# A graph network on one core: the order of work in the first blocks of each layer

## The reference

```python
for l in range(4):
    m = x @ weight[l]
    agg = segment_sum(m[src], dst)
    gi = agg @ w_ih.T + b_ih
    gh = x @ w_hh.T + b_hh
    r = sigmoid(i_r + h_r); z = sigmoid(i_z + h_z)
    n = tanh(i_n + r * h_n)
    x = (1 - z) * n + z * x
```

## Time and profile before

| | us |
|---|---|
| median of 3 runs | 2386.22 |
| lowest and highest | 2385.95, 2386.53 |
| the profiled execution | 2388.24 |
| its span in the trace | 2386.5 |
| PE busy | 2235.7 (94%) |
| DVE busy | 2227.2 (93%) |
| ACT busy | 1902.0 (80%) |
| POOL busy | 1722.0 (72%) |

### The profile page before, as it was taken

The page is one execution under the profiler, slowest core; times in us unless marked ns, Lnnn a source line. Parts: engine busy times, 40 slices in busy tenths (PEclk is TensorE's granted clock), DMA queues, the critical chain, the costliest instruction groups (busy, mean ns, idle before and its releaser), DMA issues.

```text
span 2386.5 us, 49508 instructions
## 1 busy us (share of the span) xinstructions
PE 2235.7 (94%) x11832; PEld 1888.4 (79%) x11832; DVE 2227.2 (93%) x4543; ACT 1902.0 (80%) x3592; POOL 1722.0 (72%) x1645
## 2 busy tenths in 40 slices
PE   1799999999889999999969999999979999999996
PEld 1688888888768888888858888888858888888885
DVE  7799999999879999999969999999959999999998
ACT  1588888888768888888758888888847999999996
POOL 2677778777377777777557777777658888888883
PEclk6799999999989999999989999999989999999998
DMA  2355555555535555555535555555544555555553
GB/s 56 88 158 162 158 161 159 161 157 160 150 113 170 172 172 170 173 175 169 168 109 174 171 172 171 171 172 174 167 115 127 153 151 151 151 151 151 151 151 110
DMA packets 277064, 363.68 MB, mean 152 GB/s; under 512 B 107754, under 2 KB 186586, under 8 KB 276980
## 3 DMA queue, kind: packets, MB, share of 16 engines
q1 hardware_dynamic: 238196, 310.43, 43.6%
q0 software_dynamic: 38784, 52.30, 9.1%
HBM read 209.32 MB, written 179.81 MB: 163 GB/s over the span
## 4 chain that ended last, share of the span: by engine, by line
DVE 46%; issue 28%; PE 14%; ACT 8%; DVEq 2%; DMA 1%; POOL 0%; SPq 0%; ACTq 0%; POOLq 0%
DVE a_lo L1136 8%; DVE narg L1158 8%; DVE diff L1168 5%; DVE diff L1162 5%; DVE h_lo L1129 5%; PE pR L716 4%; PE pA L704 3%; ACT pIN L882 3%; ACT pA L882 3%; PE pZ L716 3%; DVE aggT L1145 3%; DVE sel L1113 3%; DVE narg L1151 2%; DVE newT L1177 2%; PE pHN L716 2%
## 5 line engine op out<-in xcount | busy, mean ns | idle before, releaser
L569 POOL DMA_INDIRECT gath<-state,idx x900 | 941.5, 1046 | 259.9 <-issue 236.2
L549 POOL TENSOR_TENSOR h_lo<-hT,h_hi 128x252 fp32r<-128x252 f32 (+1 forms) x400 | 351.6, 879 | 256.5 <-ACT h_hi L855 171.7
L569 POOL DMA_INDIRECT gath<-in_x_dram,idx x300 | 345.9, 1153 | 108.4 <-issue 72.4
L878 ACT ACTIVATE rg<-pR,bsum 128x504 f32<-128x504 f32 x400 | 272.8, 682 | 92.4 <-PE pR L716 79.4
L1151 DVE SCALAR_TENSOR_TENSOR narg<-pHN,bhh,rg 128x504 f32<-128x504 f32 x400 | 293.7, 734 | 32.3 <-ACT rg L878 30.3
L704 PE MATMUL pA<-sel,g_hi 128*128 128x168 f32 x1200 | 279.5, 266 | 36.8 <-DVE g_lo L1124 36.8
L704 PE MATMUL pA<-sel,g_lo 128*128 128x168 f32 x1200 | 292.4, 277 | 0.0
L704 PEld LDWEIGHTS pA<-sel,g_hi 128*128 128x128 f32 x1200 | 231.9, 193 | 55.2 <-issue 38.8
L866 ACT CAST sel<-sel 128x504 fp32r (+1 forms) x400 | 246.4, 617 | 34.1 <-DVE flag_i L1120 33.9
L886 ACT ACTIVATE zg<-pZ,bsum 128x504 f32<-128x504 f32 x400 | 270.3, 676 | 0.1
L1168 DVE TENSOR_TENSOR diff<-zg,diff 128x504 f32<-128x504 f32 x400 | 268.9, 672 | 0.8 <-DVE diff L1162 0.5
(11 more groups left out here) (185 smaller groups left out, 6456.6 us busy)
## 6 DMA issues: line engine op xcount, KB each, us to landing
columns<-newT SPq DMA_DIRECT2D x300, 252.0 KB, 2.0
hT<-columns SPq DMA_DIRECT2D x300, 252.0 KB, 2.7
state<-o_rows SPq DMA_DIRECT2D x300, 224.0 KB
x_rows<-in_x_dram SPq DMA_DIRECT2D x200, 224.0 KB
out_dram<-o_rows SPq DMA_DIRECT2D x100, 224.0 KB
gath<-state,idx POOLq DMA_INDIRECT x900
state<-o_rows SPq DMA_DIRECT2D x300, 26.0 KB
idx<-edge_src SPq DMA_DIRECT2D x395, 1.5 KB
```

The lines of the kernel that those rows point to most:

```text
L549: nc.gpsimd.tensor_tensor(h_lo[:, u % RING, cols], hT[:, u % RING, cols], h_hi[:, u % RING, cols].bitcast(F32), ALU.subtract).then_inc(s_h ...
L569: pool.indirect_dma_start(out=gath[:, u % RING, j, :], out_offset=None, in_=states[l], in_offset=bass.IndirectOffsetOnAxis(ap=idx[:, u % R ...
L878: nc.scalar.activation(rg[:, :], pR[:, 0:COLS], ACT.Sigmoid, bias=bsum[:, 0:1]).then_inc(s_r, 1)
```

## The change

A constant `RAMP = 3` marks the first three blocks of each layer. In them sums, and the parts made from them, stand one block ahead; at the end of block 2 each engine makes those of block 4 besides those of block 3, and from block 3 on the distance is two, as before. PE's function of r and n products is split in two. At block 0 PE makes the state passes of r and n first, then the sums of block 0, then the three z passes on the state, then the passes on the sums; the three z passes on the sums follow behind the sums of block 1. ACT and DVE gather their parts of blocks 2 to 5 one block at a time in the same places. Code for a graph that does not fit the tables is changed in form alone and does not run here.

```diff
@@ -48,6 +48,7 @@
 OUTLAG = 9
 PRE = 3
 LATE = 2
+RAMP = 3
 
 
 V_ONEHOT = 4
@@ -717,7 +718,7 @@
                                             stop=ends and k == len(passes) - 1)
                 return last
 
-            def r_and_n_products(l, b, u, start, reused, halves, ready=1):
+            def products_on_state(l, b, u, start, halves, ready=1):
                 g = l * NB + b
                 pe.wait_ge(s_hlo, g + ready)
                 if halves:
@@ -727,7 +728,9 @@
                 product(l, u, pR[:, 0:COLS], 0, ("state",), True, False)
                 at_least(s_t1, g, start)
                 product(l, u, pHN[:, 0:COLS], 2, ("state",)).then_inc(s_HN, 1)
-                pe.wait_ge(s_alo, g + 1)
+
+            def products_on_sums(l, b, u, reused):
+                pe.wait_ge(s_alo, l * NB + b + 1)
                 product(l, u, pR[:, 0:COLS], 0, ("in",), False, True).then_inc(s_R, 1)
                 if reused is not None:
 
@@ -737,6 +740,13 @@
             def z_product(l, b, u, start):
                 at_least(s_z, l * NB + b, start)
                 product(l, u, pZ[:, 0:COLS], 1, ("in", "state")).then_inc(s_Z, 1)
+
+            def z_on_state(l, b, u, start):
+                at_least(s_z, l * NB + b, start)
+                product(l, u, pZ[:, 0:COLS], 1, ("state",), True, False)
+
+            def z_on_sums(l, u):
+                product(l, u, pZ[:, 0:COLS], 1, ("in",), False, True).then_inc(s_Z, 1)
 
             def turn_back(l, b, u, start, added=None):
                 g = l * NB + b
@@ -763,21 +773,24 @@
                         if first:
                             if l == 0:
                                 turn_h(PRE, PRE, s_xld[PRE % RING], 2, False)
+                        ramp = isinstance(i, int) and i == 0 and u < RAMP
+                        products_on_state(l, b, u, start, l < L - 1 and (l > 0 or exists_before(i, u, PRE)))
+                        if first:
                             sum_edges(l, 0, 0, start)
-                        r_and_n_products(l, b, u, start,
-                                         l * NB + b - 1 if l or exists_before(i, u, 2) else None,
-                                         l < L - 1 and (l > 0 or exists_before(i, u, PRE)))
+                            z_on_state(l, 0, 0, start)
+                        products_on_sums(l, b, u, l * NB + b - 1 if l or exists_before(i, u, 2) else None)
+                        if exists(i, u, 2):
+                            sum_edges(l, *after(i, u, 1 if ramp else 2)[:2], False)
                         if first:
-                            sum_edges(l, 1, 1, False)
-                        elif exists(i, u, 2):
-                            sum_edges(l, *after(i, u, 2)[:2], False)
-                        z_product(l, b, u, start)
-                        if first:
-                            sum_edges(l, 2, 2, False)
+                            z_on_sums(l, u)
+                        else:
+                            z_product(l, b, u, start)
                         if not first:
                             pb, pu, _ = after(i, u, -1)
                             turn_back(l, pb, pu, isinstance(i, int) and pb == 0,
                                       pb - 1 if exists_before(i, u, 3) else None)
+                        if ramp and u == RAMP - 1:
+                            sum_edges(l, RAMP + 1, RAMP + 1, False)
                         if l == 0 and exists(i, u, 4):
                             nb, nu, ni = after(i, u, 4)
                             turn_h(nb, nu, s_xld[nu % RING], 2 * (turn(ni, nu) + 1), False)
@@ -929,32 +943,34 @@
                             high_gathered(0, 0, TURNS * l + 1)
                             high_part(l, 0, 0, final)
                             high_gathered(1, 1, TURNS * l + 1)
+                        ramp = isinstance(i, int) and i == 0 and u < RAMP
                         rows(i, u)
                         r_gate(l, b, u, first and l == 0)
                         coming = on_from(l, i, u, PRE)
                         if coming:
                             nl, nb, nu, ni = coming
                             high_h(nl, nb, nu, TURNS * (nl - 1) + turn(ni, nu) + 1)
-                            if not first and nl == l:
+                            if nl == l and not ramp:
                                 high_gathered(nb, nu, TURNS * l + turn(ni, nu) + 1)
                                 if not final:
                                     widen(l, nb, nu)
+                        if ramp and u == RAMP - 1:
+                            high_gathered(RAMP + 1, RAMP + 1, TURNS * l + 1)
+                            widen(l, RAMP + 1, RAMP + 1)
                         normal(i, u, 0)
-                        if first:
-                            high_part(l, 1, 1, final)
                         n_gate(l, b, u)
-                        if not first and exists(i, u, 2):
-                            high_part(l, *after(i, u, 2)[:2], final)
+                        if exists(i, u, 2):
+                            high_part(l, *after(i, u, 1 if ramp else 2)[:2], final)
                         z_gate(l, b, u)
-                        if not first and final and exists(i, u, 3):
+                        if final and not ramp and exists(i, u, 3):
                             widen(l, *after(i, u, 3)[:2])
                         normal(i, u, 1)
-                        if first:
-                            high_gathered(2, 2, TURNS * l + 1)
-                            widen(l, 2, 2)
-                            high_part(l, 2, 2, final)
-                            high_gathered(3, 3, TURNS * l + 1)
-                            widen(l, 3, 3)
+                        if ramp:
+                            nu = u + 2 if u < RAMP - 1 else RAMP + 2
+                            high_gathered(nu, nu, TURNS * l + nu // RING + 1)
+                            widen(l, nu, nu)
+                        if ramp and u == RAMP - 1:
+                            high_part(l, RAMP + 1, RAMP + 1, final)
 
                     blocks(act, step)
                     for k in range(lag, 0, -1):
@@ -1262,7 +1278,8 @@
                         if added:
                             remainder(*after(i, u, -ROWLAG))
                             row_stats(*after(i, u, -ROWLAG)[:2])
-                        summed = after(i, u, 1 if first else 2)[:2] if exists(i, u, 2) else None
+                        ramp = isinstance(i, int) and i == 0 and u < RAMP
+                        summed = after(i, u, 1 if ramp else 2)[:2] if exists(i, u, 2) else None
                         if not final and summed:
                             aggregate(l, *summed)
                         if half:
@@ -1273,7 +1290,9 @@
                         difference(l, b, u)
                         if half:
                             squared_difference(*half)
-                        if not first and exists(i, u, 3):
+                        if ramp and u == RAMP - 1:
+                            low_gathered(l, RAMP + 1, RAMP + 1)
+                        if not ramp and exists(i, u, 3):
                             low_gathered(l, *after(i, u, 3)[:2])
                         coming = on_from(l, i, u, PRE)
                         if coming and coming[0] < L - 1:
@@ -1283,12 +1302,13 @@
                         product(l, b, u)
                         if half:
                             variance(*half)
-                        if first:
-                            low_gathered(l, 2, 2)
+                        if ramp and u < RAMP - 1:
+                            low_gathered(l, u + 2, u + 2)
+                        if ramp and u == RAMP - 1:
                             if not final:
-                                aggregate(l, 2, 2)
-                            low_part(l, 2, 2, final)
-                            low_gathered(l, 3, 3)
+                                aggregate(l, RAMP + 1, RAMP + 1)
+                            low_gathered(l, RAMP + 2, RAMP + 2)
+                            low_part(l, RAMP + 1, RAMP + 1, final)
                         if last:
                             renew(b, u, i)
```

3 lines of the change are left out of this document (2 added, 1 removed).

## The result

The changed kernel takes 2381.5 us (median of 22 runs, 2379.1 to 2384.7) against 2386.7 us (22 runs, 2384.7 to 2388.8) of the kernel before: ratio 0.9976, 95% interval 0.9971 to 0.9982, 5.2 us less. Its profiled execution took 2381.4 us with a span of 2379.7, where before's span was 2386.5; the mean granted clock is 0.972 after 0.969. The difference of the two traces is 6.8 us.

The account below looks back on a forecast made before the run. PE, DVE and clock are full except at layer changes, start and end; heads fall from 97.0 to 83.6 us, 13.4 less, minus clock costs 2.3 and 3.4: 7.7 less, 2380.5 profiled, 2378.5 us median; range 2372.0 to 2384.5.

Parts of the forecast that it names:

- the clock's first stretch: Start of each layer: PE's pause before a_lo(0) makes the clock rise later, costing 2.3 us in all.
- The wait on g_lo(2): Layer heads before the change: PE idles 4.29 us until block 2's g_lo, and the clock falls; the ramp removes this.
- the ramp's loop of 6.22 us: From narg to narg, blocks 0 to 1 and 1 to 2: 6.22 us in layers 1 and 2, 5.9 in layer 3.
- The interval from block 2 to 3, 7.78 us: Layers 1 and 2, narg to narg in the block that makes sums 3 and 4: 7.78 us.
- a_lo and product one DVE step each of 0.59: Within block 2's interval to block 3: each of these two DVE operations takes 0.59 us.
- the 9.5: Layer 3, block 2 to 3: 9.5 us, as sum(4) waits for the bank and block 3's state passes stand behind it.
- the 8.3 (7.78 + 0.54): Layer 0, block 2 to 3: 7.78 us plus 0.54 for three selections on DVE.
- The clock's fall at sum(4): After PE's wait ahead of block 4's sums: falls in layers 0 and 3, not 1 and 2; 1.7 us each, 3.4.
- The state passes of block 0 ahead of its sums I cost at nothing: Start of each layer on PE: moving block 0's state passes ahead of its sums costs nothing and gains nothing.
- gain eaten: Rival, chance 0.18: clock falls at sum(4) in all four layers, each losing 2.35 us; only 1.7 us less, 2384.5 us.
- stays low: Rival, chance 0.06: clock low all through the ramp, PE binds at 9.5 us a block; 17 us more, 2403 us.
- The gathers: Rival, chance 0.04: POOL's gathers bind from block 5 on, taking back about 1 us a layer; 3.7 us less, 2382.5 us.

Follow-up runs that it names:

- Experiment 2: Changed kernel with POOL making h_lo(4) and h_lo(5) ahead of the gathers of blocks 6 and 7; chip B, 2442.8 us, ratio 1.0027 to the kernel before.
- experiment 6: Kernel of experiment 5 with block 3's six state passes ahead of sum(4) on TensorE; chip A, 2376.3 us, ratio 0.9958 to the kernel before.
- experiment 5: Changed kernel with POOL's h_lo(5) waiting for block 2's product instead of block 1's; chip A, 2379.6 us, ratio 0.9970 to the kernel before.
- experiment 7: Changed kernel with block 0's state passes back in their old place, ramp kept; chip A, 2380.6 us, ratio 0.9973 to the kernel before.
- experiment 3: Changed kernel with 24 unread TensorE passes added behind block 0's state passes in layers 1 to 3; chip B, 2444.5 us, ratio 1.0036 to the kernel before.
- Experiment 9: Changed kernel with POOL's h_lo in every block waiting for the block's own diff; chip C, 2638.5 us in one run, 216 more than the kernel before.
- experiment 8: On chip C, experiment 6 unchanged: 2423.3 us, ratio 0.9994 to the kernel before; with a_hi(4), a_lo(4) moved into block 3 in layers 0 to 2: 2421.9, 0.9995.

## Why the prediction was right, and where it was not

The total came 3.0 us above the forecast of 2378.5, inside its range, and 0.24% faster than before, a little over the 0.2% that can be told. Of the 3.0 us, 2.1 come from the step from the profiled execution to the median: the forecast took 2.0 us off (2380.5 to 2378.5), as before's profiled execution lay above its median, but the new one took 2381.4 us and the median is 2381.5. The remaining 0.9 us is small partly by luck: layers 1 and 2 took 1.0 us each more than forecast from block 0 to block 3 (21.2 for 20.2) and layer 0 0.4 more (24.0 for 21.9 + 1.7), while layer 3, whose clock did not fall, took 1.9 less (21.1 for 21.3 + 1.7); and 1.2 us that were not foreseen behind block 3 stand against 0.9 too many for the clock's first stretch. Step by step:

- **The heads and the loop: right.** The wait on g_lo(2) was what TensorE lost, and the ramp's loop of 6.22 us measured 6.20, 6.19, 6.18 and 6.18 in layers 1 and 2, in layer 3 5.84 and 5.83 (5.9), in layer 0 6.81 and 6.55 (6.76). Single steps were off by up to 0.07 us, in both directions.
- **The interval from block 2 to 3, 7.78 us: right for what it counted, short by one mechanism.** Experiment 2 measured 7.81 where nothing disturbs it, and experiment 6, with another order on TensorE, 7.75. In the changed kernel it is 8.85, as the step "a_lo and product one DVE step each of 0.59" failed: POOL's h_lo(5), which stands behind a gather in POOL's list, lies across them in the ramp; experiments 2 and 5 moved it and both were short again. In layer 3 the 9.5 were right without a fall (9.48). In layer 0 the 8.3 (7.78 + 0.54) were 0.9 short: experiment 7, where its clock stayed up, has 9.22. The 0.9 us is what VectorE's h_lo loses there (1.33 for 0.41), and experiment 6, where it is short, has 8.32; that this is the cause was not tested alone.
- **The clock's fall at sum(4): the size was right, the place was not.** A fall costs 1.6 us in layer 3 (11.05 - 9.48), 1.4 in layer 0 (10.66 - 9.22); I had 1.7. But the step "I let the clock fall in layers 0 and 3 and not in 1 and 2" rested on the length of the wait, and that does not decide. In the six traces with sum(4) in this place (the changed kernel twice, experiments 2, 3, 5 and 7) it fell in layers 0 to 3 in 5, 5, 4 and 1 of them. The waits ahead were 2.2, 1.7, 1.7 and 2.4 us: the longest was the safest, and the same program with the same wait fell in one execution and not in the next. Experiment 9's trace, where POOL's order is another, has one more fall in its four layers, in layer 0, and none behind 1.69 and 1.95 us of wait in layers 2 and 3.
- **The clock's fall and the held operations do not add up.** Layers 1 and 2, from block 2 to 3: neither 7.75 to 7.81 us; held operations alone 8.85; fall alone 8.92 to 9.67; both 8.86 to 9.66. They are two paths to the same r gate, over ScalarE's queue and over TensorE, and the later one counts. That fits with experiment 5, which removed one and gave 3.0 us with intervals that overlap, and 6, which removed both and gave 6.3, some of it by the order alone, as said there.
- **The clock's first stretch: 1.4 us against 2.3**, but by experiment 7, where the sum of the same four stretches is 1.6 us above before's, even that is no effect of the moved passes. From last to first narg single traces scatter with the same code: by 0.6 us in the changed kernel, and by 1.6 in layer 3 of the ramp of one block (21.40 and 22.97).
- **"The state passes of block 0 ahead of its sums I cost at nothing": right**, by experiment 7.
- **Missing: 1.2 us behind block 3**, 0.5 of it the one interval of layer 2 that follows its fallen clock.

Of the rivals, "gain eaten" lost, since it wanted four falls of 2.35 us, and so did "stays low", which is also where the Trainium skill pointed ("TensorE: Matmul & The Clock Gate", section "HAM oscillation"): its mechanism is there, falls behind waits of 1.7 to 2.4 us in 15 of 24 places, and with the wait cut to 1.02 us or less there was none (12 places in the three traces of experiments 6 and 8), but a fall lasts under 4 us, not the whole ramp. The waits in that section's own case are longer than the ramp's ahead of sum(4), so it did not say as much as the rival took from it. The gathers bound nothing: in the changed kernel's trace ScalarE's g_hi waits for a gather three times in the later layers, once at each layer's block 0, as it must.

**What stays open.** What ends the remote waits of chips B and C, and so why kernels with the ramp of three, which saves 5 us on chip A, were level or behind there, was not settled; there is no trace of the kernel before on these chips, and the changed kernel itself was not run on them. The ramp of one block was not run on chip A. Why layer 3's longer wait seldom brings the clock down is not known. Of the kernels run, experiment 6 is the best on chip A and the ramp of one block on chips B and C.

## What to carry to other kernels

When a reordering changes how far ahead one engine's queue runs, look up what moves beside it on the others: here the steps of the critical loop could be added up from start times to 0.02 us, though single steps were off by up to 0.07, and the largest error within the trace, apart from the clock, came from an off-path instruction that slid beside the path. Put work that is ready ahead of an instruction that waits: with six passes moved into a wait of 1.7 us the clock also stayed up there in every layer. And compare kernels only on one chip: the 0.4% that experiment 6 gained on chip A was none on chip C.
